# Running the expert router inside the feed-forward block instead of in a block ahead of it

## The reference

```python
def _L0_ffn_ref(x, router_W, router_b, sW1, sb1, sW2, sb2, eW1, eb1, eW2, eb2):
    shared = jax.nn.relu(xt @ sW1 + sb1) @ sW2 + sb2
    logits = xt @ router_W + router_b
    probs = jax.nn.softmax(logits / T, axis=-1)
    top_p, top_i = jax.lax.top_k(probs, K)          # K = 3 of E = 15
    cw = cw.at[jnp.arange(n)[:, None], top_i].set(top_p)
    h = jax.nn.relu(jnp.einsum('nd,edh->neh', xt, eW1) + eb1)
    ye = jnp.einsum('neh,ehd->ned', h, eW2) + eb2
    routed = jnp.einsum('ned,ne->nd', ye, cw)
    return shared + routed

x = x + 0.5 * _L0_ffn_ref(_layernorm(x, axis=-1), ...)
x = x + _L0_attn_ref(_layernorm(x, axis=-1), ...)
x = x + 0.5 * _L0_ffn_ref(_layernorm(x, axis=-1), ...)
```

## Time and profile before

| | us |
|---|---|
| runs of the kernel before (2) | 5549.14 and 5804.01, median 5676.57 |
| the profiled execution | 4994.17 |
| its span, core 6, the slowest | 4992.6 |
| spans of the other cores | 4963.5 to 4990.4 |
| mean granted TensorE clock of the cores | 0.908 to 0.913 |
| TensorE idle before L591, released by the DMA of the shared weights | 46.0 in 2 waits |
| ScalarE idle before L437 (the exponential) | 169.5 in 2 waits |

### The profile page before, as it was taken

How to read it: one execution, slowest core, us unless ns; L and a number is a source line. 1 busy time by engine, 2 the same in 40 slices (tenths; PEclk the granted TensorE clock), 3 DMA queues, 4 the chain that set the end, 5 groups by cost and what they waited for, 6 DMA issues and landing times. The chain is left out here.

```text
span 4992.6 us, 55367 instructions; the slowest of 8 cores (4963.5 to 4992.6 us)
## 1 busy us (share of the span) xinstructions
PE 4269.9 (86%) x21809; PEld 1984.4 (40%) x21809; DVE 1525.0 (31%) x1742; ACT 883.0 (18%) x934; POOL 282.2 (6%) x184
## 2 busy tenths in 40 slices
PE   1199999999999999934677672599999999999998
PEld 0044444444444444412233330244444444444443
DVE  3512222222222222253342346222222222222222
ACT  1011111111111111111332331111111111111111
POOL 0200000000000000011220121000000000000000
PEclk8599999999999999967667666799999999999999
DMA  3222322222222222104214210322222222222221
GB/s 83 43 44 40 48 45 39 39 43 39 39 39 39 39 39 39 20 18 68 34 34 68 38 31 17 54 39 38 41 53 42 52 43 39 38 39 48 46 39 70
DMA packets 97077, 212.79 MB, mean 43 GB/s; under 512 B 3829, under 2 KB 3829, under 8 KB 94002
## 3 DMA queue, kind: packets, MB, share of 16 engines
q0 software_dynamic: 86192, 177.64, 21.2%
q1 hardware_dynamic: 10632, 31.61, 2.1%
HBM read 369.54 MB, written 8.57 MB: 76 GB/s over the span
## 5 line engine op out<-in xcount | busy, mean ns | idle before, releaser
L591 PE MATMUL ff_pA<-zT,ff_w 128*128 128x512 bf16 (+1 forms) x4608 | 959.2, 363 | 46.0 <-DMA ff_w<-sW 46.0
L613 PE MATMUL ff_pB<-ff_g,ff_w 128*128 128x512 bf16 (+1 forms) x4608 | 954.6, 361 | 0.0
L613 PE MATMUL ff_pA<-ff_g,ff_w 128*128 128x512 bf16 (+1 forms) x4608 | 954.5, 361 | 0.0
L591 PE MATMUL ff_pB<-zT,ff_w 128*128 128x512 bf16 (+1 forms) x4608 | 954.4, 361 | 0.0
L662 DVE TENSOR_TENSOR ff_g<-ff_r,ff_c 128x1024 bf16<-128x1024 bf16 (+1 forms) x480 | 340.3, 709 | 1415.1 <-ACT ff_r L648 1415.1
L648 ACT ACTIVATE ff_r<-ff_pA,eb1c 128x1024 bf16<-128x1024 f32 (+1 forms) x240 | 273.9, 1141 | 2302.8 <-PE ff_pA L591 2302.8
L591 PEld LDWEIGHTS ff_pA<-zT,ff_w 128*128 128x128 bf16 x4608 | 430.1, 98 | 533.7 <-issue 54.1
L613 PEld LDWEIGHTS ff_pA<-ff_g,ff_w 128*128 128x128 bf16 x4608 | 428.8, 98 | 485.1 <-issue 4.6
L613 PEld LDWEIGHTS ff_pB<-ff_g,ff_w 128*128 128x128 bf16 x4608 | 428.5, 98 | 485.9 <-issue 6.2
L591 PEld LDWEIGHTS ff_pB<-zT,ff_w 128*128 128x128 bf16 x4608 | 429.0, 98 | 483.7
L671 DVE TENSOR_TENSOR R<-ff_pA,R 128x1024 f32<-128x1024 f32 (+1 forms) x256 | 322.1, 1258 | 721.0 <-PE ff_pA L613 509.6
(11 more groups left out here) (132 smaller groups left out, 1761.5 us busy)
## 6 DMA issues: line engine op xcount, KB each, us to landing
ff_w<-eW POOLq DMA_DIRECT2D x60, 2048.0 KB, 16.9
ff_c<-scr_cwt SPq DMA_DIRECT2D x45, 256.0 KB, 3.3
ff_w<-sW POOLq DMA_DIRECT2D x4, 2048.0 KB, 23.4
at_wA<-WkT POOLq DMA_DIRECT2D x4, 2048.0 KB, 17.6
at_wB<-WvT POOLq DMA_DIRECT2D x4, 2048.0 KB, 27.2
at_wA<-WqT POOLq DMA_DIRECT2D x4, 2048.0 KB, 14.7
at_wB<-WoT POOLq DMA_DIRECT2D x4, 2048.0 KB, 14.1
R<-xT SPq DMA_DIRECT2D x1, 4352.0 KB
```

The lines of the kernel that those rows point to most:

```text
L591: mm = t.matmul(bank[:, to:to + tn], wb[m1 % 3][:, c, dh * P:(dh + 1) * P], zT[:, c, cl0 + ho + to: cl0 + ho + to + tn], start=(c == 0), s ...
L613: mm = t.matmul(bank[:, to:to + tn], wb[m2 % 3][:, dh, do * P:(do + 1) * P], gbuf[:, dh, to:to + tn], start=(dh == 0), stop=last)
```

## The change

The router's own block is gone. `phase_router` became `make_router`, which opens its buffers in the feed-forward's scope and returns one function for each engine; `phase_ffn` calls these inside its own block. SyncE, ScalarE and VectorE run their router part first. TensorE computes the logits first, then the first eight first-layer groups of the shared expert, and then the transposes, ahead of the first second-layer group. One more wait stands ahead of the first matmul that reads `cwx`. GpSimd's list has no router part. The logits and the transposes now have one PSUM buffer each instead of two, and VectorE copies a transposed chunk from PSUM straight to bf16 in `cwx`, so that the float32 rows and the one large cast are gone. The router has semaphores of its own (`s_rpe`, `s_rdv`, `s_rac`). Its selection chain is unchanged.

```diff
-        def phase_router(cl0, cln, cwf, cwx, tapap):
+        def make_router(cl0, cln, cwf, cwx, ps):
...
-                prtA = ps.enter_context(nc.psum_tensor(f"rt_pA{u}", [P, NE], F32))
-                prtB = ps.enter_context(nc.psum_tensor(f"rt_pB{u}", [P, NE], F32))
-                ptwA = ps.enter_context(nc.psum_tensor(f"rt_tA{u}", [NE, P], F32))
-                ptwB = ps.enter_context(nc.psum_tensor(f"rt_tB{u}", [NE, P], F32))
+            prt = ps.enter_context(nc.psum_tensor(f"rt_p{u}", [P, NE], F32))
+            ptw = ps.enter_context(nc.psum_tensor(f"rt_t{u}", [NE, P], F32))
...
+            def pe_logits(t):
+                for k in range(nch):
+                    if k >= 1:
+                        t.wait_ge(s_rdv.h, dve0r + k)
+                    for c in range(DC):
+                        mm = t.matmul(prt[:, :], zT[:, c, cl0 + k * P: cl0 + (k + 1) * P],
+                                      rWb[:, c, :], start=(c == 0), stop=(c == DC - 1))
...
+            def pe_trans(t):
+                t.wait_ge(s_rdv.h, dve1r + 2)
+                for k in range(nch):
+                    if k >= 1:
+                        t.wait_ge(s_rdv.h, dve2r + k)
+                    t.transpose(ptw[0:NE, :], cwf[:, k, :], identf[:, :]).then_inc(s_rpe.h, 1)
...
-                            v.tensor_copy(cwT32[0:NE, cl0 + k * P: cl0 + (k + 1) * P], ptw[0:NE, :])
-                            v.drain()
-                            v.nop().then_inc(s_dve.h, 1)
-                        v.tensor_copy(cwx[0:NE, cl0:cl0 + cln], cwT32[0:NE, cl0:cl0 + cln])
+                for k in range(nch):
+                    v.wait_ge(s_rpe.h, pe1r + k + 1)
+                    v.tensor_copy(cwx[0:NE, cl0 + k * P: cl0 + (k + 1) * P], ptw[0:NE, :])
+                    v.drain()
+                    v.nop().then_inc(s_rdv.h, 1)
...
+                rt = make_router(cl0, cln, cwf, cwx, ps)
                 pe0, act0, dve0 = s_pe.n, s_act.n, s_dve.n
...
                     @blk.sync
                     def _(sy):
+                        rt["sync"](sy)
...
                     @blk.tensor
                     def _(t):
+                        rt["pe_logits"](t)
+                        ebwait = [True]
...
                                     gidx += 1
+                                if ei == 0 and hf == 0:
+                                    rt["pe_trans"](t)
                                 if hf == 0:
                                     t.wait_ge(s_wm[m2 % 3].h, wtgt[m2])
...
                                     if ei == 0:
+                                        if ebwait[0]:
+                                            t.wait_ge(s_rdv.h, rt["cwx_ev"])
+                                            ebwait[0] = False
...
                     @blk.scalar
                     def _(s):
+                        rt["act"](s)
...
                     @blk.vector
                     def _(v):
+                        rt["dve"](v)
...
-                phase_router(0, TX, cwf, cwx, t_cw1)
                 if upto >= 3:
-                    phase_ffn(0, TX, [(0, 1152), (1152, 1024)], cwx)
+                    phase_ffn(0, TX, [(0, 1152), (1152, 1024)], cwf, cwx)
```

More of the change, by code:

```diff
@@ L126, in build_program @@
         s_gp = Ctr(es, nc, "s_gp")
+        s_rpe = Ctr(es, nc, "s_rpe")
+        s_rdv = Ctr(es, nc, "s_rdv")
+        s_rac = Ctr(es, nc, "s_rac")
         def tap3(tapap, sbap):
@@ L472, in phase_router @@
-            if tapap is not None:
-                tap3(tapap, cwf[:, :, :])
-        def phase_ffn(cl0, cln, halves, cwx):
+            prt = ps.enter_context(nc.psum_tensor(f"rt_p{u}", [P, NE], F32))
+            ptw = ps.enter_context(nc.psum_tensor(f"rt_t{u}", [NE, P], F32))
+            logt = ps.enter_context(nc.sbuf_tensor(f"rt_lg{u}", [P, NCH, NE], F32))
+            probs = ps.enter_context(nc.sbuf_tensor(f"rt_pr{u}", [P, NCH, NE], F32))
+            tt1 = ps.enter_context(nc.sbuf_tensor(f"rt_t1{u}", [P, NCH, NE], F32))
@@ new lines, in make_router @@
+            nmx = ps.enter_context(nc.sbuf_tensor(f"rt_nm{u}", [P, 1], F32))
+            f17 = ps.enter_context(nc.sbuf_tensor(f"rt_f17{u}", [P, NCH], F32))
+            r17 = ps.enter_context(nc.sbuf_tensor(f"rt_r17{u}", [P, NCH], F32))
+            iota15m = ps.enter_context(nc.sbuf_tensor(f"rt_iom{u}", [P, NE], F32))
+            pe0r, dve0r, act0r = s_rpe.n, s_rdv.n, s_rac.n
+            dve1r = dve0r + nch
+            dve2r = dve1r + 2
+            pe1r = pe0r + nch
+            st = {"cwx_ev": dve2r + nch + 1}
@@ new lines, in make_router @@
+            T1f = tt1.ap().rearrange("p a b -> p (a b)")[:, 0:nf]
+            CWf = cwf.ap().rearrange("p a b -> p (a b)")[:, 0:nf]
+            io_b = iota15.ap().unsqueeze(1).broadcast_to((P, nch, NE))
+            iom_b = iota15m.ap().unsqueeze(1).broadcast_to((P, nch, NE))
+            def pe_logits(t):
[5 more added lines that the diff above has]
+                                      rWb[:, c, :], start=(c == 0), stop=(c == DC - 1))
+                        if c == DC - 1:
+                            mm.then_inc(s_rpe.h, 1)
+                s_rpe.n += nch
@@ new lines, in act, with sync @@
+            def act(sc):
+                sc.wait_ge(s_rdv.h, dve1r + 1)
+                sc.activation(PRf, Lf, AF.Exp, bias=nmx[:, 0:1]).then_inc(s_rac.h, 1)
+                s_rac.n += 1
+            def sync(sy):
+                sy.wait_ge(s_rdv.h, st["cwx_ev"])
+                sy.dma_start(scr_cwt[:, cl0:cl0 + cln], cwx[0:NE, cl0:cl0 + cln]).then_inc(s_hw.h, 16)
+                s_hw.n += 16
+                sy.wait_ge(s_hw.h, s_hw.n)
+            return {"pe_logits": pe_logits, "pe_trans": pe_trans, "dve": dve,
+                    "act": act, "sync": sync, "cwx_ev": st["cwx_ev"]}
@@ L476, in phase_ffn @@
+        def phase_ffn(cl0, cln, halves, cwf, cwx):
             uid[0] += 1
@@ L1061, in _ @@
                         g.wait_ge(s_in.h, s_in.n)
-                phase_router(0, TX, cwf, cwx, t_cw1)
                 if upto >= 3:
-                    phase_ffn(0, TX, [(0, 1152), (1152, 1024)], cwx)
+                    phase_ffn(0, TX, [(0, 1152), (1152, 1024)], cwf, cwx)
+                    if t_cw1 is not None:
+                        tap3(t_cw1, cwf[:, :, :])
             if upto >= 3 and t_y1 is not None:
@@ L1087, in _ @@
                         g.wait_ge(s_in.h, s_in.n)
-                phase_router(HALO, TOWN, cwf, cwx, t_cw3)
-                phase_ffn(HALO, TOWN, [(0, 1024), (1024, 1024)], cwx)
+                phase_ffn(HALO, TOWN, [(0, 1024), (1024, 1024)], cwf, cwx)
+                if t_cw3 is not None:
+                    tap3(t_cw3, cwf[:, :, :])
         with nc.Block() as blk:
```

192 lines of the change are left out of this document (63 added, 129 removed).

## The result

The changed kernel took 4941.98 us at the median of 11 runs. The kernel before, timed beside it and before it, took 5305.38 at the median of 10 runs, with its four lowest between 4988.98 and 4991.92. In some runs of either kernel a whole die has a lower granted clock and takes longer (5654.19 us with one die at 0.79, for 4941.98 with all cores near 0.92), and the ratios here compare undisturbed runs with undisturbed runs. That ratio is 0.9902, interval 0.9889 to 0.9915: the change is worth 1.0% and lies within 2%. Taken on the profiled execution's 4994.17 us, 0.9902 is 48.9 us, and the ends of the interval are 42 and 55; the prediction's sum was 48.5. The profiled execution of the changed kernel took 4941.36 us, 52.8 less.

A forecast was written before the change was run, and what follows sets the result against it. TensorE, busy 86% of the span, was taken as the bound, with only 121.7 us ahead of the dense parts open to change. 84.39 - 31.12 - 4.76 = 48.5 us saved; 5676.57 - 48.5 = 5628 us, range 5440 to 5802.

The forecast's parts named there:

- part 1: Ahead of both feed-forward phases: first weight loads issue with the router's start, 43.32 and 41.07 us earlier, together 84.39.
- part 2: Router logits: one PSUM buffer gives a 0.99 us pitch, costing nothing because logits end 2.0 us before the weights land.
- part 3: Top-3 selection on VectorE: runs beside TensorE's first eight groups, ready near 222.2, with 13.7 us of slack.
- part 4: Transposes between first and second layer: on TensorE's path at 0.98 us each, costing 16.05 and 15.07 us, together 31.12.
- Rival B: Transposes: exchange nearer 0.52 us and the clock holds, so 67 us are saved, 5610; chance 0.10.
- part 5: Second layer's start: clock falls during the transposes, adding a cold start of 2.45 and 2.31 us, together 4.76.
- Rival C: Second layer: clock falls in the transposes and stays down, making the kernel 124 us slower, 5801; chance 0.04.
- Rival A: First weight load: VectorE's logit-stage work stretches it, losing 6.4 us over both phases, saving 42, 5635; chance 0.10.
- Rival D: Weight loads: still wait for the router's end, so only the transposes' extra price or about zero, 5677; chance 0.06.

The follow-up runs named there:

- the two-buffer kernel: The changed kernel with two PSUM buffers for the transposes, the logits keeping one; ratio 0.9874 to the kernel before.
- the spread one: The changed kernel with single transposes behind TensorE's groups from the seventh first-layer group on, second biases moved to expert 1; ratio 0.9840 to the kernel before.
- the kernel with more copies: The changed kernel with one unused 128x1152 bf16 VectorE copy behind each logit add; ratio 0.9899 to the kernel before.

## Why the prediction was right, and where it was wrong

The working of the saving held; the absolute time and its range did not. That the saving came out at 48.9 by the ratio for a sum of 48.5 is closer than the measurement can tell: the interval reaches from 42 to 55 us, and the two spans differ by 52.8.

**The level was wrong.** The step that failed is "so I carry the saving over in microseconds: 5676.57 - 48.5 = 5628", and with it the range, whose ends were the two runs of before shifted. I had noted that no row of the trace holds the 13.7% between the profiled execution and the median of the two runs, and built on the median all the same. Of the ten runs of before now known, four lie within 3 us of each other near 4990, where the profiled execution of 4994.17 lies too; the two that I built on lie 556 and 812 us above the lowest of them, and what held them there is not on record for these two runs. The sum against the profiled execution, 4945.7, is within 0.1% of the 4941.98 measured.

**Term by term** (us; expected, then read from the rows above):

| | expected | measured |
|---|---|---|
| router's first matmul to first expert matmul, phase 1 | 18.2 | 18.49 |
| the same, phase 2 (0.48 + the old load's 18.62) | 19.1 | 17.66 |
| pitch of the logit chunks | 0.99 | 0.87, 0.90 on average |
| end of the selection, after the router's first matmul | 38.2 | 36.5 |
| transposes, phase 1 and 2 | 16.05, 15.07 | 15.46, 14.89 |
| added by the cold second layer, phase 1 and 2 | 2.45, 2.31 | 1.61, 2.42 |

Added up over both phases from the same rows, the first expert matmul came 85.6 us earlier (84.4 expected), the transposes cost 30.4 (31.1), the cold second layer 4.0 (4.8), and the first layers took 0.2 us more than before. That makes 50.9 us for the 48.5 of the sum.

- *The loads start with the router* (part 1): right. The lag of GpSimd was 0.43 and 0.40 us for the 0.48 taken. Taking away the early load alone, back to the selection's end, costs 71 us.
- *The logits' second buffer* (part 2): right that it costs nothing, and measured by giving it back. The pitch was read too high: 0.99 was the first round trip of the phase, which also stood behind VectorE's two small scalings; the steady one is 0.87. The cover was 3.7 us for the 2.0 expected.
- *The selection is hidden* (part 3): right, with a slack of 15.2 us for the 13.7 expected.
- *The transposes* (part 4): right. The mechanism is shown by the two-buffer kernel (14 us) and by the spread one. Rival B, that they run nearer 0.52, is refuted: warm, the pitch was still 0.88, because only the 0.10 us of the transpose itself went with the clock.
- *The clock* (part 5): it fell and came back as expected. Rival C, that it stays down, is refuted: the second of the new groups is at full pace. Its price was also set a little high: in the second half of the tokens a group takes 3.45 us and not 3.90.
- *Rival A*, the loads stretched by VectorE: refuted for this kernel. The first expert matmul came 18.06 us after the issue, 0.3 more than the 17.74 of before, where A asked for 3.2 more. The rule of the Trainium skill in "SBUF — State Buffer", section "SBUF: two separate sides", is about operations of VectorE that take both ports, and about the writing of the descriptors, and it is not tested by this. No row shows whether the logit adds are such operations, though the prediction counted them all. If the descriptors are written in GpSimd's three issues (2.7 us, no data moving yet), only one copy of the kernel with more copies lay beside them. The 60 expert loads that the prediction set against the rule do not settle it either: they show that data moves at full pace beside VectorE.
- *Rival D*: refuted by GpSimd's row at 186.03.

The spans differ by 52.8 us, the two stretches by 50.9. The other 1.9 us lie outside them, most of all between the two, where TensorE's lists are alike: from 283.82 to 3127.98 it took 2844.2 us before, from 259.00 to 3099.62 it took 2840.6. On four cores of each kernel this stretch lies between 2834.3 and 2844.2 us, so a difference of 1.9 says nothing.

## What to carry to other kernels

When a wait for data stands behind a stretch of work that doesn't need the data, what pays is to issue the load earlier; merging the blocks did nothing by itself. Work that is moved beside a dense stretch should be checked for the piece that needs the dense engine itself: here 33 tiny transposes, run in two rows, cost 30 us and two cold starts of 4 us together; at the 0.11 us that one costs alone between two groups they come to an estimated 3.6. And when the runs that set a level lie far from the profiled execution with nothing in the trace to show for it, settle what they are before an absolute time is built on them.

## What the runs showed that I had not expected

- A pair of engines that hand one small tile back and forth has a pitch that hardly depends on TensorE's clock: 0.88 us at 2.4 GHz and 0.98 at 1.2 GHz with one buffer, 0.51 with two.
- The clock fell some 5 us into the transposes, with TensorE at work about a third of the time. With two buffers it fell as well, and the next group took 6.00 us for 4.58 in the kernel before.
- The price of a cold start varies by itself: the first group of the first layer took 6.35 and 5.77 us before, 5.96 and 6.41 after the change.
- The first quarter of a weight matrix, rows of 256 columns, landed soon enough for an expert matmul 8.8 us after the router's first one; with the whole matrix it came 17.7 to 18.5 us after.
- VectorE's work beside GpSimd's issues became longer and the issues did not: 0.67 us for a copy that took 0.46 elsewhere.
